# Identity products of TensorE in the first waits of six stages, and a tanh feed-forward stage that works on raw x with centred weights

## The chip, the cores and the metric

One core of a Trainium2 chip. A core has five engines that run their own instruction streams and meet through semaphores: TensorE (PE, matrix products; its weight loads are PEld in the profile), VectorE (DVE), ScalarE (ACT), GpSimd (POOL) and SyncE (SP, which only issues DMAs here). Operands lie in SBUF, products land in PSUM. The metric is the device time of one launch in microseconds; lower is better.

## The reference, cut to what matters

A residual stream `x` of 8 x 1024 tokens by 256 channels passes through eight sublayers, each fed with a layernorm of x without gain or offset. The change touches the arithmetic of the two tanh sublayers alone:

```python
def _layernorm(x, axis=-1, eps=1e-05):
    m = jnp.mean(x, axis=axis, keepdims=True)
    v = jnp.var(x, axis=axis, keepdims=True)
    return (x - m) / jnp.sqrt(v + eps)

def _L1_ffn_ref(x, weight, aux_weight1, aux_weight2, bias):
    h = jnp.einsum('btc,cd->btd', x, weight)
    h = jnp.einsum('btc,cd->btd', h, aux_weight1)
    h = jnp.einsum('btc,cd->btd', h, aux_weight2)
    return jnp.tanh(h + bias)

x = x + _L0_attn_a_ref(_layernorm(x), ...)   # local attention
x = x + _L0_ffn_ref(_layernorm(x), ...)      # top-k experts
x = x + _L0_attn_b_ref(_layernorm(x), ...)   # spectral attention
x = x + _L0_ffn_ref(_layernorm(x), ...)      # top-k experts again
x = x + _L1_attn_a_ref(_layernorm(x), ...)   # second-order attention
x = x + _L1_ffn_ref(_layernorm(x), ...)      # tanh stage, t6
x = x + _L1_attn_b_ref(_layernorm(x), ...)   # window attention
x = x + _L1_ffn_ref(_layernorm(x), ...)      # tanh stage, t8
```

Everything is float32.

## The kernel before, in words

x stays in SBUF as `R.X`, 64 tiles (NT) of 128 tokens by 256 channels. `hybrid_kernel` (L2627) calls one function for each sublayer, and a stage begins only when all engines have left the one before: each `nc.Block()` ends with all engines meeting. The statistics of each tile (`bn_stats` into `R.raw`) are taken by the stage that last writes it; the next stage turns them into `R.rstd` and `R.shift` in `layernorm_scales` (L73) on VectorE, with one square root on ScalarE (`std_of_var`, L91).

`tanh_ffn` (L149) runs twice, as `t6` and as `t8`, which also stores the output. Head of the stage: SyncE loads three 256x256 weights and the bias (L184, L185), all on one semaphore, `loaded`. TensorE waits for all four (L195), transposes the first weight into `psW` (L198), and multiplies twice (L209), so that `wc` holds the product of the three; ScalarE copies `psW` to SBUF between the steps (L236). Then come the 64 tiles. For each, VectorE normalizes the tile into `xn` (L259), TensorE transposes its two halves (L218) into one of two banks `psT`, ScalarE copies them to `xnT` (L242), TensorE multiplies them with `wc` (L226) into one of four banks `psY`, VectorE adds the bias (L266), ScalarE takes tanh (L248), GpSimd adds the result to x (L278), and in t6 VectorE takes the statistics (L270). `skewed` (L31) writes each engine's order: transposes of tile i, then products of tile i-2; on VectorE normalize i, bias i-3, stats i-7. The first and last tiles are written out, those between are a loop of four tiles with indices in registers. A float32 product of TensorE is two records in the trace, a transpose one.

The stages whose beginnings the change touches: the experts' second half (`top_k_experts`, L283; TensorE's order at L615), which waits for gathered rows (L581) and then multiplies (L596) for ScalarE's gelu (L644); `turned_copies` (L713), called only as `ww` for the weights of the window stage (transposes L739, copies L746); `spectral_attention` (L749), whose first products are L904 and which transposes its weights at L915; `second_order_attention` (L1463), which begins with a transpose (L1566) and products (L1573); `window_attention` (L1878), which begins with transposes of normalized tiles (L2017). In each of these TensorE's first instruction is a wait for a load or for a first tile.

## Time and profile before

| | us |
|---|---|
| median of 3 runs | 3975.1 (3974.56 to 3976.0) |
| the profiled execution | 3985.05 |
| span of its instructions | 3983.0 |
| PE busy in it | 3608.2 (91%) |
| DVE busy | 2388.3 (60%) |
| ACT busy | 2058.1 (52%) |
| POOL busy | 1351.3 (34%) |

Times in rows of the profile are microseconds from the start of the span; 2.05 us of the execution lie around the span. A row of the timeline gives the start, the duration, the engine, the line, the operation, what is written and what is read, how many were merged (x4), and in brackets how long the engine had stood idle and what ended that.
### The profile page before, as it was taken

Reading aid. Unit: us, or ns where it says so; the run is one execution under the profiler, and the core shown is the slowest. Engines: PE = TensorE matmul, PEld = TensorE weight load, DVE = VectorE, ACT = ScalarE, POOL = GpSimd, SP = SyncE. Lnnn points to the kernel's source line nnn. Section 1 sums busy time; section 2 is a strip of 40 time slices with the busy share of each in tenths; the row PEclk is TensorE's granted clock in tenths of the full one; section 3 lists DMA queues with packets and bytes.
Section 4 is the critical chain, followed back from the end, with each engine's and each line's share of the span. In section 5 each row is a group of like instructions: output and inputs, shape, how many; then the busy total and the mean of one; then the engine's idle time right before and its main releaser. Section 6 shows DMA issues by size and latency. Waiting matters only on the chain. (4 is left out here: it accounts for less than half of the span.)

```text
span 3983.0 us, 116418 instructions
## 1 busy us (share of the span) xinstructions
PE 3608.2 (91%) x44602; PEld 3108.5 (78%) x44602; DVE 2388.3 (60%) x6575; ACT 2058.1 (52%) x6294; POOL 1351.3 (34%) x1988
## 2 busy tenths in 40 slices
PE   8939999699739996999999999999987999999988
PEld 7829999577529996888888888888864777777766
DVE  6774554688665555344444444444446888888885
ACT  3335554455345552343434434444333788888884
POOL 3435565101036553333333333333324122222114
PEclk9969999899969998999999999999988999999998
DMA  3134444212144335000000000000000000000002
GB/s 116 44 132 99 90 95 95 86 48 61 49 151 92 90 78 135 2 3 3 3 3 3 3 3 3 3 3 2 3 11 15 2 2 2 2 2 2 2 2 94
DMA packets 137694, 162.36 MB, mean 41 GB/s; under 512 B 11329, under 2 KB 127969, under 8 KB 137185
## 3 DMA queue, kind: packets, MB, share of 16 engines
q1 hardware_dynamic: 112608, 121.71, 9.5%
q0 software_dynamic: 24576, 33.57, 4.9%
q8 instruction: 355, 5.82, 0.6%
q14 instruction: 155, 1.26, 0.1%
HBM read 96.39 MB, written 58.85 MB: 39 GB/s over the span
## 5 line engine op out<-in xcount | busy, mean ns | idle before, releaser
L2142 ACT ACTIVATE wa_S<-wa_S,wa_top 128x256 f32<-128x256 f32 x1024 | 511.6, 506 | 138.1 <-DVE wa_top L2206 137.2
L1801 DVE TENSOR_TENSOR so_AB<-so_rows,so_masks 128x1024 f32<-128x1024 f32 x256 | 313.6, 1225 | 246.4 <-PE so_rows L1545 227.4
L2206 DVE CUSTOM_DVE_ANT_0 wa_S<-wa_bank,wa_band 128x256 f32<-128x256 f32 x1024 | 366.9, 420 | 7.4 <-issue 7.3
L1860 POOL TENSOR_TENSOR so_state<-so_compact,so_head 128x384 f32<-128x384 f32 x224 | 185.1, 826 | 339.5 <-PE so_bankC L1612 248.3
L1790 DVE SCALAR_TENSOR_TENSOR so_compact<-so_compact,so_bankX 128x96 f32<-128x96 f32 x192 | 48.9, 255 | 414.2 <-PE so_bankX L1648 414.2
L2068 PE MATMUL wa_bank<-ident,wa_S 128*128 128x128 f32 x2048 | 275.1, 276 | 20.9 <-ACT wa_probT L2149 20.9
L2068 PEld LDWEIGHTS wa_bank<-ident,wa_S 128*128 128x128 f32 x2048 | 231.2, 141 | 66.0 <-ACT wa_S L2142 29.5
L1573 PE MATMUL so_bankJ<-so_xnT,so_w 128*128 128x128 f32 x2048 | 253.3, 278 | 1.2 <-ACT so_QT L1710 0.7
L1573 PEld LDWEIGHTS so_bankJ<-so_xnT,so_w 128*128 128x128 f32 x2048 | 242.1, 194 | 1.9 <-ACT so_QT L1710 1.0
L1736 ACT COPY so_OT<-so_bankC 128x128 f32<-128x128 f32 x256 | 68.1, 266 | 307.7 <-PE so_bankC L1612 307.7
L1855 POOL TENSOR_TENSOR so_Ug<-so_U,so_decay_t 128x128 f32<-128x128 f32 x224 | 102.1, 456 | 325.4 <-ACT so_U L1723 325.4
L644 ACT ACTIVATE m4e_hT<-m_bank,m4e_bias 128x256 fp32r<-128x256 f32 x256 | 127.4, 498 | 153.7 <-PE m_bank L596 147.9
L644 ACT ACTIVATE m2e_hT<-m_bank,m2e_bias 128x256 fp32r<-128x256 f32 x256 | 125.9, 492 | 149.5 <-PE m_bank L596 143.0
L2142 ACT ACTIVATION_READ_ACCUMULATOR wa_S<-wa_S,wa_top 128x1 f32 x1024 | 199.2, 195 | 0.0
L2214 DVE COPY wa_probT<-wa_bank 128x512 f32<-128x512 f32 x256 | 167.0, 687 | 48.0 <-PE wa_bank L2068 46.7
L596 PE MATMUL m_bank<-m2e_exT,m_w_parts 128*128 128x256 f32 x1536 | 190.7, 284 | 0.0
L596 PE MATMUL m_bank<-m4e_exT,m_w_parts 128*128 128x256 f32 x1536 | 190.1, 283 | 0.3 <-ACT m4e_h L644 0.3
L610 PE MATMUL m_bank<-m_w_parts,m4e_hT 128*128 128x256 f32 x1536 | 189.5, 282 | 0.6 <-DVE m4e_pre L691 0.6
L610 PE MATMUL m_bank<-m_w_parts,m2e_hT 128*128 128x256 f32 x1536 | 189.5, 282 | 0.6 <-DVE m2e_pre L691 0.6
L610 PEld LDWEIGHTS m_bank<-m_w_parts,m4e_hT 128*128 128x128 f32 x1536 | 186.3, 189 | 0.8 <-issue 0.8
L610 PEld LDWEIGHTS m_bank<-m_w_parts,m2e_hT 128*128 128x128 f32 x1536 | 186.3, 189 | 0.8 <-issue 0.8
L596 PEld LDWEIGHTS m_bank<-m2e_exT,m_w_parts 128*128 128x128 f32 x1536 | 185.1, 191 | 0.0
(427 smaller groups left out, 9889.4 us busy)
## 6 DMA issues: line engine op xcount, KB each, us to landing
m_w_raw<-in_L_ffn_W_dram SPq DMA_DIRECT2D x64, 512.0 KB, 3.7
sum_dram<-X SPq DMA_DIRECT2D x16, 1024.0 KB, 4.8
X<-sum_dram SPq DMA_DIRECT2D x16, 1024.0 KB, 7.3
X<-in_L_attn_a_x_dram SPq DMA_DIRECT2D x8, 1024.0 KB, 11.6
xn_dram<-m2r_xn SPq DMA_DIRECT2D x16, 512.0 KB, 3.1
sp_gx<-gate_dram SPq DMA_DIRECT2D x64, 128.0 KB, 2.9
xn_dram<-m4r_xn SPq DMA_DIRECT2D x16, 512.0 KB, 3.1
out_dram<-X SPq DMA_DIRECT2D x8, 1024.0 KB, 4.4
```

Source lines behind the costliest of these rows:

```text
L596: last = nc.tensor.matmul(bank[:, 0:2 * P], w_parts[:, par, a, c, f * P:(f + 1) * P], exT[:, s % 2, b, c], start=(n == 0), stop=(n == len( ...
L610: last = nc.tensor.matmul(by[u][:, 0:HID], hT[:, s % 2, a, f, u * P:(u + 1) * P], w_parts[:, par, b, 2 + f // QF, f % QF * HID:(f % QF + 1 ...
L644: last = nc.scalar.activation(to, bh[f % 4][:, 0:2 * P], ACT.Gelu_apprx_tanh, bias=bias[:, par, f:f + 1])
L1573: last = nc.tensor.matmul(bJ[:, k * P:(k + 1) * P], w[:, n, c, k * P:(k + 1) * P], xnT[:, c * P:(c + 1) * P], start=(c == 0), stop=(c == H ...
L1736: nc.scalar.copy(OT[:, t % (2 * UT)], bC[:, P:2 * P]).then_inc(s_["O_ready"], 1)
L1801: nc.vector.tensor_tensor(AB[:, t % 2].rearrange("p h m t -> p h (m t)"), rows4[:, :, 0:2 * P], masks[:].rearrange("p m t -> p (m t)")[:, ...
L1855: nc.gpsimd.tensor_tensor(Ug[:, t % 2], U[:, t % 2], decay_t[:], ALU.mult).then_inc(s_["Ug_ready"], 1)
L1860: nc.gpsimd.tensor_tensor(state[:, t % UT], compact[:, t % UT, :, None, :].broadcast_to([P, 3, HG, DK]), head[:, None, :, None].broadcast_ ...
L2068: last = nc.tensor.transpose(bT[q % 2][:, (2 * h + k) * P:(2 * h + k + 1) * P], S[:, n % 2, 2 * q + h, k * P:(k + 1) * P], R.ident[:])
L2142: nc.scalar.activation(S[:, n % 2, z], S[:, n % 2, z], ACT.Exp, bias=top[:, n % 2, z:z + 1], scale=-1.0, accum_out=sums[:, i % 2, SET * c ...
L2206: nc.vector.tensor_tensor_reduce(out=S[:, n % 2, z], in0=bS[g][:, eo * SPAN:(eo + 1) * SPAN], in1=band[:], scale=-(D ** -0.5), scalar=3e38 ...
L2214: nc.vector.tensor_copy(probT[:, n % 2, 2 * q:2 * q + 2].rearrange("p h k t -> p (h k t)"), bT[q % 2][:]).then_inc(s_["T_dve"], 1)
```

## The change

A helper, `keep_busy`, issues products of the 128x128 identity with itself into a bank that isn't in use yet. It is called as TensorE's first work in the experts' second half (30 products), in `turned_copies` (12), in the spectral (13), second-order (30) and window stage (30), and twice in the head of a tanh stage (6 and 4).

The tanh stage no longer normalizes x. The mean over its input channels is taken out of each column of the first weight (`off`, added while `psW` is copied to `wT`, now by VectorE), so that raw x times these weights equals centred x times the old ones; the division by the deviation is done behind the product, where VectorE multiplies by `R.rstd` and adds the bias in one operation. TensorE transposes tiles of `R.X` as they stand, from the block's beginning, in the order turn 0, fillers, weight transposes, turn 1, fillers, first weight product, turn 2, second, turn 3, then for each i products i and turn i+4. There are three banks for transposes and three for products (before two and four). Each weight has its own semaphore, and the bias is waited for by VectorE alone. All 64 tiles are written out, with no loop in registers.

```diff
@@ -93,6 +93,12 @@
     nc.scalar.activation(R.var[:], R.var[:], ACT.Sqrt).then_inc(std_ready, 1)
 
 
+def keep_busy(nc, R, bank, count):
+
+    for _ in range(count):
+        nc.tensor.matmul(bank[:, 0:P], R.ident[:], R.ident[:], start=True, stop=True)
+
+
...
 
 
@@ -151,6 +157,7 @@
     def sem(name):
         return sem_(f"{tag}_{name}")
 
+    RING, AHEAD = 4, 4
...
@@ -162,27 +169,29 @@
         wT = sb("wT", [P, HC, HID])
         w01T = sb("w01T", [P, HC, HID])
         wc = sb("wc", [P, HC, HID])
+        off = sb("off", [P, HC])
         bias_all = sb("bias_all", [P, HID])
-        xn = sb("xn", [P, 4, HID])
-        xnT = sb("xnT", [P, 4, HC, P])
+        xT = sb("xT", [P, RING, HC, P])
         pre = sb("pre", [P, 4, HID])
         th = sb("th", [P, 4, HID])
-        psT = [ps(f"psT{i}", [P, 512]) for i in range(2)]
-        psY = [ps(f"psY{i}", [P, 512]) for i in range(4)]
+        psT = [ps(f"psT{i}", [P, 512]) for i in range(3)]
+        psY = [ps(f"psY{i}", [P, 512]) for i in range(3)]
         psW = ps("psW", [P, HC, HID])
 
...
 
         with nc.Block() as block:
             @block.sync
             def _(sp):
                 for n, src in enumerate((weight, aux1, aux2)):
-                    sp.dma_start(w[:, n], src.rearrange("(c p) d -> p c d", p=P)).then_inc(loaded, 16)
-                sp.dma_start(bias_all[:], bias.rearrange("(a d) -> a d", a=1).broadcast_to([P, HID])).then_inc(loaded, 16)
+                    sp.dma_start(w[:, n], src.rearrange("(c p) d -> p c d", p=P)).then_inc(w_loaded[n], 16)
+                sp.dma_start(bias_all[:], bias.rearrange("(a d) -> a d", a=1).broadcast_to([P, HID])).then_inc(bias_loaded, 16)
...
@@ -191,93 +200,112 @@
 
             @block.tensor
             def _(pe):
-
-                pe.wait_ge(loaded, 64)
+                def turn(i):
+                    if i >= len(psT):
+                        pe.wait_ge(xT_ready, i - len(psT) + 1)
+                    for c in range(HC):
+                        last = nc.tensor.transpose(psT[i % len(psT)][:, c * P:(c + 1) * P], R.X[:, i, c * P:(c + 1) * P], R.ident[:])
+                    last.then_inc(psT_ready, 1)
+
+                def products(i):
+                    pe.wait_ge(xT_ready, i + 1)
+                    if i >= len(psY):
+                        pe.wait_ge(pre_ready, i - len(psY) + 1)
+                    for c in range(HC):
+                        last = nc.tensor.matmul(psY[i % len(psY)][:, 0:HID], xT[:, i % RING, c, :], wc[:, c, :], start=(c == 0), stop=(c == HC - 1))
+                    last.then_inc(psY_ready, 1)
+
+                turn(0)
+                keep_busy(nc, R, psY[0], 6)
+                pe.wait_ge(w_loaded[0], 16)
                 for c in range(HC):
                     for h in range(HC):
                         last = nc.tensor.transpose(psW[:, h, c * P:(c + 1) * P], w[:, 0, c, h * P:(h + 1) * P], R.ident[:])
                 last.then_inc(wstep, 1)
-                for m, (lhs, rhs) in enumerate(((1, wT), (2, w01T))):
-
-                    pe.wait_ge(wcopied, m + 1)
-                    for o in range(HC):
-                        for c in range(HC):
-                            if m == 0:
-                                a, b = w[:, 1, c, o * P:(o + 1) * P], wT[:, c, :]
-                            else:
-                                a, b = w01T[:, c, o * P:(o + 1) * P], w[:, 2, c, :]
-                            last = nc.tensor.matmul(psW[:, o, :], a, b, start=(c == 0), stop=(c == HC - 1))
-                    last.then_inc(wstep, 1)
-                pe.wait_ge(wcopied, 3)
-
-                def transposes(i, s):
-                    pe.wait_ge(xn_ready, i + 1)
-                    if past(i, 2):
-                        pe.wait_ge(xnT_ready, i - 1)
+                turn(1)
+                keep_busy(nc, R, psY[0], 4)
+                pe.wait_ge(w_loaded[1], 16)
+                pe.wait_ge(wT_ready, HC)
+                for o in range(HC):
                     for c in range(HC):
...
-                    last.then_inc(psT_ready, 1)
-
-                def products(i, s):
-                    pe.wait_ge(xnT_ready, i + 1)
-                    if past(i, 4):
-                        pe.wait_ge(pre_ready, i - 3)
+                        last = nc.tensor.matmul(psW[:, o, :], w[:, 1, c, o * P:(o + 1) * P], wT[:, c, :], start=(c == 0), stop=(c == HC - 1))
+                last.then_inc(wstep, 1)
+                turn(2)
+                pe.wait_ge(w_loaded[2], 16)
+                pe.wait_ge(wcopied, 1)
+                for o in range(HC):
                     for c in range(HC):
-                        last = nc.tensor.matmul(psY[s][:, 0:HID], xnT[:, s, c, :], wc[:, c, :], start=(c == 0), stop=(c == HC - 1))
-                    last.then_inc(psY_ready, 1)
-
-                skewed(pe, NT, [(0, transposes), (2, products)], unroll=4)
+                        last = nc.tensor.matmul(psW[:, o, :], w01T[:, c, o * P:(o + 1) * P], w[:, 2, c, :], start=(c == 0), stop=(c == HC - 1))
+                last.then_inc(wstep, 1)
+                turn(3)
+                pe.wait_ge(wcopied, 2)
+                for i in range(NT):
+                    products(i)
+                    if i + AHEAD < NT:
+                        turn(i + AHEAD)
 
             @block.scalar
             def _(act):
+                def copy_xT(i):
+                    act.wait_ge(psT_ready, i + 1)
+                    if i >= RING:
+                        act.wait_ge(psY_ready, i - RING + 1)
+                    nc.scalar.copy(xT[:, i % RING].rearrange("p c t -> p (c t)"), psT[i % len(psT)][:, 0:HID]).then_inc(xT_ready, 1)
+
+                def tanh(i):
+                    act.wait_ge(pre_ready, i + 1)
+                    if i >= 4:
+                        act.wait_ge(x_ready, i - 3)
+                    nc.scalar.activation(th[:, i % 4], pre[:, i % 4], ACT.Tanh).then_inc(th_ready, 1)
+
                 std_of_var(nc, act, R, var_ready, std_ready)
-                for m, dst in enumerate((wT, w01T, wc)):
-                    act.wait_ge(wstep, m + 1)
-                    nc.scalar.copy(dst[:], psW[:]).then_inc(wcopied, 1)
-
...
+                copy_xT(0)
+                copy_xT(1)
+                act.wait_ge(wstep, 2)
+                nc.scalar.copy(w01T[:], psW[:]).then_inc(wcopied, 1)
+                copy_xT(2)
+                act.wait_ge(wstep, 3)
+                nc.scalar.copy(wc[:], psW[:]).then_inc(wcopied, 1)
+                copy_xT(3)
+                for i in range(NT):
+                    if i + AHEAD < NT:
+                        copy_xT(i + AHEAD)
+                    tanh(i)
 
             @block.vector
             def _(dve):
                 layernorm_scales(nc, dve, None, R, step, var_ready, std_ready)
-
-                def normalize(i, s):
-                    if past(i, 4):
-                        dve.wait_ge(psT_ready, i - 3)
-                    nc.vector.tensor_scalar(xn[:, s], row_of(R.X, i), R.rstd[:, bass.ds(i, 1)], R.shift[:, bass.ds(i, 1)],
-                                            ALU.mult, ALU.add).then_inc(xn_ready, 1)
-
-                def add_bias(i, s):
+                dve.wait_ge(wstep, 1)
+                nc.vector.tensor_reduce(off[:], psW[:], AX_X, ALU.add).then_inc(centred, 1)
+                dve.wait_ge(centred, 1)
+                nc.vector.tensor_scalar(off[:], off[:], -1.0 / HID, None, ALU.mult).then_inc(centred, 1)
+                dve.wait_ge(centred, 2)
+                for h in range(HC):
+                    nc.vector.tensor_scalar(wT[:, h, :], psW[:, h, :], off[:, h:h + 1], None, ALU.add).then_inc(wT_ready, 1)
+                dve.wait_ge(bias_loaded, 16)
+
+                def add_bias(i):
                     dve.wait_ge(psY_ready, i + 1)
-                    if past(i, 4):
+                    if i >= 4:
                         dve.wait_ge(th_ready, i - 3)
-                    nc.vector.tensor_tensor(pre[:, s], psY[s][:, 0:HID], bias_all[:], ALU.add).then_inc(pre_ready, 1)
-
-                def stats(i, s):
+                    nc.vector.scalar_tensor_tensor(out=pre[:, i % 4], in0=psY[i % len(psY)][:, 0:HID], scalar=R.rstd[:, i:i + 1],
+                                                   in1=bias_all[:], op0=ALU.mult, op1=ALU.add).then_inc(pre_ready, 1)
+
+                def stats(i):
                     dve.wait_ge(x_ready, i + 1)
-                    nc.vector.bn_stats(row_of(R.raw, i), row_of(R.X, i))
-
-                skewed(dve, NT, [(0, normalize), (3, add_bias)] + ([(7, stats)] if out is None else []), unroll=4)
+                    nc.vector.bn_stats(R.raw[:, i, :], R.X[:, i, :])
+
+                for i in range(NT + 4):
+                    if i < NT:
+                        add_bias(i)
+                    if out is None and i >= 4:
+                        stats(i - 4)
 
             @block.gpsimd
             def _(pool):
-                def residual(i, s):
+                for i in range(NT):
                     pool.wait_ge(th_ready, i + 1)
-                    nc.gpsimd.tensor_tensor(row_of(R.X, i), row_of(R.X, i), th[:, s], ALU.add).then_inc(x_ready, 1)
-
-                skewed(pool, NT, [(0, residual)], unroll=4)
+                    nc.gpsimd.tensor_tensor(R.X[:, i, :], R.X[:, i, :], th[:, i % 4], ALU.add).then_inc(x_ready, 1)
 
 
 def top_k_experts(nc, R, tag, A, C, before):
@@ -612,6 +640,7 @@
                                                         start=(n == 0), stop=(n == len(steps) - 1))
                         last.then_inc(down_done, 1)
 
+                    keep_busy(nc, R, ban[5], 30)
                     skewed(pe, PAIRS, [(0, turn_x), (1, up), (2, down)], unroll=U)
 
                 @block.scalar
@@ -731,6 +760,7 @@
 
             @block.tensor
             def _(pe):
+                keep_busy(nc, R, banks[0], 12)
                 pe.wait_ge(loaded, 16 * len(jobs))
                 for n, (parts, _) in enumerate(blocks):
                     if n >= 2:
@@ -1058,6 +1088,7 @@
                     pe.wait_ge(L_copied, u + 1)
                     nc.tensor.transpose(yb[1][:, HID:HID + P], turned_L[:], R.ident[:]).then_inc(LT_done, 1)
 
+                keep_busy(nc, R, fb[0], 13)
                 pe.wait_ge(c_loaded, 48)
                 for b in range(2):
                     for n in range(TB // 2):
@@ -1649,6 +1680,7 @@
                                                 V[:, tile(t) % 2, t % UT, head_rows(h)], start=True, stop=True, tile_position=(0, h * DK))
                     last.then_inc(s_["S_done"], 1)
 
+                keep_busy(nc, R, bC, 30)
                 pe.wait_ge(s_["loaded"], 9 * 16)
                 turn_x(0)
                 project(0, 0)
@@ -1997,6 +2029,7 @@
 
             @block.tensor
             def _(pe):
+                keep_busy(nc, R, bO, 30)
                 pe.wait_ge(s_["loaded"], 5 * 16)
                 pe.wait_ge(s_["zeroed"], 5)
 
```

## Rows read from the trace of the kernel before

**Rows 1.** The page: TensorE's granted clock in 40 slices, tenths.

```profile
PEclk9969999899969998999999999999988999999998
```

**Rows 2.** Stretches of the tanh loops: length, busy PE, PEld, DVE, ACT, POOL, then PEclk, DMA.

```profile
2958.13:3038.43 80.30, 75.24 (x375) 54.82 (x375) 65.53 (x180) 43.69 (x125) 43.55 (x60) 0.99 0.00 0
3900.37:3975.35 74.98, 74.44 (x375) 55.52 (x375) 51.16 (x122) 43.70 (x125) 43.59 (x60) 0.99 0.29 98
```

**Rows 3.** Timeline: head of t6, and t8's first product.

```profile
2940.27 0.38 SPq L184 DMA_DIRECT2D t_w<-in_L_ffn_weight_dram  x1
...
2945.74 1.11 PE L198 MATMUL t_psW<-ident,t_w 128*128 128x128 f32 x4 [9.50 <-DMA t_bias_all<-in_L_ffn_bias_dram]
2946.89 0.58 ACT L236 COPY t_wT<-t_psW 128x512 f32<-128x512 f32 x1 [4.43 <-PE t_psW L198]
...
2947.53 3.78 PE L209 MATMUL t_psW<-t_wT,t_w 128*128 128x256 f32 x8 [0.67 <-ACT t_wT L236]
...
2958.13 1.91 PE L226 MATMUL t_psY<-t_wc,t_xnT 128*128 128x256 f32 x4
...
3900.37 1.92 PE L226 MATMUL t_psY<-t_wc,t_xnT 128*128 128x256 f32 x4
```

**Rows 4.** DMA issues in the head: size, median us to landing.

```profile
t_w<-in_L_ffn_weight_dram SPq DMA_DIRECT2D x1, 256.0 KB, 2.8
```

**Rows 5.** Timeline: products of neighbouring tiles, and of t6's last three.

```profile
2961.31 1.03 PE L226 MATMUL t_psY<-t_wc,t_xnT 128*128 128x256 f32 x4
...
2962.40 1.03 PE L226 MATMUL t_psY<-t_wc,t_xnT 128*128 128x256 f32 x4
...
3036.71 2.76 PE L226 MATMUL t_psY<-t_wc,t_xnT 128*128 128x256 f32 x12
```

**Rows 6.** Waits in t6's loop: total us, times, longest.

```profile
PEld t_psT L218 <- DVE t_xn L259: 12.2, 39, 0.6
```

**Rows 7.** Groups of instructions: count, busy us, mean ns, idle before.

```profile
L1372 DVE SCALAR_TENSOR_TENSOR sp_late<-sp_gx,sp_bank 128x256 f32<-128x256 f32 x64 | 25.8, 420 | 20.4 <-PE sp_bank L1023 19.5
...
L436 DVE TENSOR_REDUCE m2r_Lsum<-m2r_L 128x64 f32<-128x512 f32 x1 | 0.7, 686 | 0.0
```

**Rows 8.** Short stretches, columns as in the group of the tanh loops.

```profile
2960.00:2962.00 2.00, 2.00 (x13) 1.74 (x11) 1.45 (x4) 0.84 (x3) 0.00 (x0) 0.95 0.00 0
...
753.00:757.00 4.00, 0.19 (x2) 0.00 (x0) 0.61 (x2) 4.00 (x9) 0.00 (x0) 0.77 0.00 0
...
735.00:737.00 2.00, 2.00 (x20) 2.00 (x19) 1.83 (x4) 1.42 (x3) 2.00 (x17) 1.00 0.00 0
```

**Rows 9.** Timeline: beginnings of the other stages, first real work of each.

```profile
296.21 0.20 DVE L667 TENSOR_SCALAR m2e_bias<-m_b 128x8 f32<-128x8 f32 x1 [2.23 <-PEq L118]
...
306.12 1.12 PE L581 MATMUL m_bank<-ident,m2e_ex_in 128*128 128x128 f32 x4 [13.21 <-DMA m2e_ex_in<-xn_dram,m2e_rows]
...
716.72 0.27 DVE L77 TENSOR_TENSOR mean<-raw 128x64 f32<-128x64 f32 x1 [2.60 <-PEq L118]
...
722.44 6.39 PE L904 MATMUL sp_bank<-sp_dft,sp_xn 128*128 128x128 f32 x32 [30.54 <-ACT sp_xn L1130]
...
733.40 5.84 PE L915 MATMUL sp_bank<-ident,sp_late 128*128 128x128 f32 x52
...
1580.36 0.27 DVE L77 TENSOR_TENSOR mean<-raw 128x64 f32<-128x64 f32 x1 [2.60 <-PEq L118]
...
1590.88 0.66 PE L1566 MATMUL so_bankJ<-ident,so_xn 128*128 128x128 f32 x2 [35.34 <-POOL so_xn L1840]
...
1592.06 3.79 PE L1573 MATMUL so_bankJ<-so_xnT,so_w 128*128 128x128 f32 x16 [0.52 <-ACT so_xnT L1703]
...
3042.00 0.37 SPq L730 DMA_DIRECT2D ww_staged<-in_L_attn_b_Wqkv_dram  x1
...
3047.48 3.76 PE L739 MATMUL wa_bank<-ident,ww_staged 128*128 128x128 f32 x16 [8.01 <-DMA ww_staged<-in_L_attn_b_Wout_dram]
...
3063.69 2.20 PE L2017 MATMUL wa_bank<-ident,wa_xn 128*128 128x128 f32 x8 [12.45 <-POOL wa_xn L1961]
```

22 lines of the change are left out of this document (6 added, 16 removed).

## The prediction

> **What bounds the kernel now.** I read the page's clock line first [rows 1], and its busy shares, then the busy table of the two tanh stages [rows 2], then the beginning of the first of them instruction by instruction [rows 3, 4], then two neighbouring tiles and the last ones [rows 5], then the waits [rows 6]. TensorE carries the kernel: it is at full clock in most slices, and busy for 91% of the span, so time is won where TensorE waits, or where it works at 1.2 GHz instead of 2.4. The diff touches both.
>
> In a tanh stage the two windows of rows 2 run from the first product of tile 0 to the first product of tile 63. The end points are worked out from the timeline: 2958.13 and 3900.37 begin the first products [rows 3], and the last three tiles are one run of twelve records from 3036.71 [rows 5], of which the last tile has four, so tile 63 begins 8 x 0.215 = 1.72 us later, at 3038.43. (The second stage's 3975.35 is read in the same way.) So 63 tiles take 80.3 us in the first stage (1.27 us each) and 75.0 us in the second (1.19). VectorE is busy for 65.5 and 51.2 us of them, ScalarE for 43.7, GpSimd for 43.6 [rows 2]. VectorE has three operations per tile in the first stage (normalize, add bias, stats) and register work between them; TensorE's weight loads wait 12.2 us for the normalized tile there, the largest wait of TensorE in the loop [rows 6]. Where TensorE isn't held up, as in the tiles before the loop, a tile takes 1.085 us from products to products (2961.31 to 2962.40, and the pair before it alike) [rows 5]: 4 x 0.215 for the products, the rest for two transposes.
>
> The head of the stage is a chain: loads issued at 2940.27, TensorE's first work at 2945.74 (it waits for the bias, which it doesn't need), transposes, copy, 3.78 us of products, copy, 3.78 us, copy, the first transposes of x, the first product at 2958.13 [rows 3]. All of it runs at 1.2 GHz; the clock comes back at about 2960.1 (0.95 granted in 2960 to 2962) [rows 8].
>
> **The tanh stages, per tile.** *Normalize* leaves VectorE: 64 operations, and their register work and waits. The bias addition becomes one operation that multiplies by the reciprocal deviation and adds. No such instruction with this shape reads a product here; the nearest, a three-operand one of 128x256 with one operand in PSUM, takes 0.42 us [rows 7], what the addition takes now. I take 0.42; even at 0.5 VectorE would have 0.92 us per tile with the stats, under TensorE's 1.085. ScalarE keeps a copy and a tanh (43.7/63 = 0.69 us) and GpSimd its addition (43.6/60 = 0.73) [rows 2]. So the next bound is TensorE's own 1.085 us. The new order puts the transposes of tile i+4 behind the products of tile i, with four turned tiles kept; the copy that a product needs was then issued three tiles earlier, over 3 us, which covers copy plus tanh. The last four tiles have no transposes: 0.86 each. From product 0 to product 63: 60 x 1.085 + 3 x 0.86 = 67.7 us, against 80.3 and 75.0: 12.6 and 7.3 us less. The tail behind the last product (bias, tanh, addition, store or stats) stays.
>
> **The tanh stages, head.** The bias no longer gates. The first weights land 2.8 us after issue [rows 4], at 2943.1. Till then TensorE turns tile 0 (0.45) and runs 6 fillers. A filler is a 128-column product in two records; at 1.2 GHz sixteen such records take 3.79 us with their end [rows 9], so a filler is about 0.43 us, at 2.4 GHz 0.215. 2940.3 + 0.45 + 2.6 = 2943.3. The four transposes of the weights end at 2944.5. The copy is replaced on VectorE by a reduction of 512 values (0.69 [rows 7]), a scaling (0.2, as small operations of VectorE take, 0.20 and 0.27 in rows 9) and two shifts of 0.42, with hand-overs 1.9 us instead of 0.58; its scales are done before. TensorE fills this with tile 1 and 4 fillers (2.2 us): first weight product at 2946.5, 1.0 us earlier than now. By then TensorE has worked some 6 us almost unbroken. Now TensorE's bursts have pauses of 0.67 us between them, and the clock rises only behind three of them [rows 3, 8]; I expect it up by about 2947. Then both products of weights take 2.1 instead of 3.78, the copies 0.65 each: 2946.5 + 2 x (2.1 + 0.68) = 2952.1, and product 0 follows at once, since tiles 0 to 3 are turned in the gaps. That is 6.0 us before 2958.13. If the clock stays low it is 2946.5 + 2 x (3.78 + 0.68) = 2955.4, 2.7 us. I take 6.0 in both stages.
>
> Tanh stages together: 12.6 + 7.3 + 12.0 = **31.9 us**.
>
> **The fillers of the other stages.** They gain only if the clock is still up when real work comes, if that work is bound by TensorE, and if they end before it. What fillers leave behind counts: from 753.2 TensorE stands still, and in 753 to 757 the grant averages 0.77, so it fell at about 755.2, 2 us after the last product [rows 8].
> - *Experts* (30 fillers, twice): block from 296.2, data at 306.12 [rows 9]. At 1.2 GHz throughout the fillers take 12.9 us and end 3 us late; with the rise after some 5 us they end near 305.1, with a pause of 1 us, the transposes (1.12 us at low clock) and again 1.6 us of waiting for VectorE. The clock will probably drop again in there. Sure is half of the transposes, 0.6 us. Behind them ScalarE's gelu is late, not TensorE. 0.6 each, bounds -2.9 and +1.5.
> - *Spectral* (13 fillers): 716.7 + 5.6 = 722.3 before 722.44 [rows 9]. Here the filler joins the work with hardly a pause, which is the good case: 32 records take 6.39 us, and would take 3.2 at 2.4 GHz. ScalarE and VectorE, which supply and empty, would hold them up then, and the clock still needs its first microseconds. 1.5 us, bounds 0 and 2.5.
> - *Second-order* (30): block from 1580.36, tile ready at 1590.88. Ends near 1589, then a pause of up to 2 us and bursts with waits. If the clock held, the 3.79 us of products at 1592.06 would halve, their equal twins behind them too, and the first round of the stage's small products with them, 5.5 us together; if it falls, 0 to 0.9. 0.8, bounds -2.2 and 5.5.
> - *Window weights* (12): 3042.0 + 5.2 = 3047.2, data used at 3047.48: almost no pause. Sixteen records take 3.76 us; ScalarE's copies of 0.59 come next, so 0.7, bounds -0.5 and 1.
> - *Window* (30): the tile comes 12.45 us after TensorE's last work [rows 9], a change of blocks included; its transposes are paced by GpSimd. 0.2, bounds -2 and 2.2.
>
> These sum to 1.2 + 1.5 + 0.8 + 0.7 + 0.2 = **4.4 us**.
>
> The Trainium skill (TensorE: Matmul & The Clock Gate, "Why this matters for your kernels") asks only that there be no long idle gaps between bursts. By that the pauses of 1 to 2 us behind the fillers would cost nothing, and second-order and window stages would gain their upper bounds. The 2 us of rows 8 speak against it, so I give that a rival and not the sum. The same page ("PE-mode transpose") states that transposes don't count as activity; the transposes from 733.40 run at 1.00 in 735 to 737 [rows 8, 9], so the trace doesn't bear that out, at least for holding the clock.
>
> **Sum.** 31.9 + 4.4 = 36.3 us. The profiled execution took 3985.05 us: 3948.7 there. The median, 3975.1, is 0.25% below it, so 3975.1 - 36.3 = **3938.8 us**.
>
> **Rivals.**
> 1. *The fillers hold the clock up into the real work* in second-order and window stages: +4.7 and +2.0. 3932. For it: only pauses of 1 to 2 us. Against: 755.2. Chance 0.13.
> 2. *The tile period stays near 1.19.* If something other than normalize sets the second stage's pace (TensorE is busy there for 74.4 of 75.0 us [rows 2], so it may simply be slower in long runs), the loop gains 5.3 and 0 instead of 12.6 and 7.3: 14.6 less, 3953. Against: the undisturbed tiles at 1.085. 0.12.
> 3. *The change doesn't do what it says*: fillers don't lift the clock. Heads 2.7 each (6.6 less), the other gains gone (4.4), and the long fillers end late: 2 x 2.9 + 2.2 + 2 = 10.0. Gain 15.3: 3960. Against: matrix products raise it everywhere else. 0.04.
> 4. *Slower than before*: the in-order queues close into a ring. ScalarE's copy for tile i+4 stands ahead of tanh i, TensorE's turn waits for a copy, and if that slack of three tiles isn't there a tile costs products, bias, tanh and copy in series: 1.03 + 0.42 + 0.42 + 0.37 = 2.2 us. 126 tiles x (2.24 - 1.085) = 146 less 36: 4085. It decides from a period of 1.085 + 36.3/126 = 1.37 on. Against: each wait reaches back three or four tiles. 0.02.
>
> The forecast itself has 0.69. Its own spread: heads 2.7 to 6.5, period 1.07 to 1.11 (3 us), and the spectral stage, where the clock falls and returns on its own; moving the start can add or remove a few such falls at 1.7 us each, so +-4. That gives 3931 to 3947.
>
> **Numbers.** 3938.8, range 3929 to 3952: it takes in rival 1 and leaves out half of 2, and 3 and 4. A measurement of this kernel tells about 0.2%, 8 us, from no change. Faster by more: 0.96; within: 0.02; slower: 0.02.
>
> **What would show it.** Right: products of neighbouring tiles 1.08 to 1.09 us apart in both stages and TensorE's wait for x gone; product 0 about 12 us after the first load's issue, with a grant of 1.00 by then; no idle of TensorE between fillers and the weights' transposes. Fillers: grant 1.00 at the end of each run, and 0.50 again while the second-order stage's first products run; if 1.00 there, rival 1. A period of 1.19 makes rival 2. The prediction is wrong if a real first instruction stands behind a running filler, or if TensorE waits for ScalarE's copy in the tanh loop.

## The result, and the profile after

The changed kernel takes 3945.57 us (median of 4 runs, 3944.08 to 3946.38), the kernel before 3975.55 beside it: a ratio of 0.9924, with a 95% interval from 0.9907 to 0.9941. That is 30.0 us less. The forecast had 3938.8, in a range from 3929 to 3952, and 36.3 less. The profiled executions differ by more than the medians: 3985.05 us before and 3945.89 after, 39.2 less. Where these 9 us come from is half of what follows.

The page of the changed kernel, its shares of busy time and TensorE's granted clock by slice:

```profile
PE 3624.8 (92%) x44932; PEld 3148.0 (80%) x44932; DVE 2352.1 (60%) x6455; ACT 2063.0 (52%) x6292; POOL 1352.5 (34%) x1988
...
PEclk9969999899969998999999999999999999999999
```

Beside [rows 1], the two 8s at three quarters of the span and the one at the end have gone. A slice is 99.6 us there. The first (2888 to 2987 us) and the last (from 3883) hold the heads of the two tanh stages, the second (2987 to 3087) the beginning of the window stage.

The table of busy time by stretch (start and end, length, busy PE, PEld, DVE, ACT, POOL with counts, PEclk, DMA share, GB/s) for the two tanh loops, again from the first product of tile 0 to the first of tile 63:

```profile
2943.00:3010.73 67.73, 67.73 (x372) 58.34 (x373) 49.23 (x120) 44.96 (x124) 44.08 (x61) 1.00 0.00 1
3868.68:3936.41 67.73, 67.73 (x372) 58.33 (x373) 30.00 (x62) 44.89 (x124) 44.03 (x61) 1.00 0.33 109
```

Against [rows 2] the stretches shrank from 80.30 and 74.98 to 67.73 us each: 12.57 and 7.25 less. TensorE is busy in all of it. In the waits of the first stretch no wait of TensorE for x or for its copy is left; VectorE, ScalarE and GpSimd now wait for TensorE or for each other. The columns are engine and line, what it waited for, total us, times, longest:

```profile
POOL X L308 <- ACT t_th L259: 43.9, 58, 23.8
DVE t_pre L291 <- PE t_psY L215: 24.0, 61, 6.8
ACT t_xT L253 <- PE t_psT L207: 21.6, 57, 1.2
...
PE t_psY L215 <- ACT t_wc L268: 0.5, 1, 0.5
```

The timeline of the first tanh stage's head (start, length, engine, line, operation, and in brackets the idle time before it and what ended it), to be read beside [rows 3]:

```profile
2931.86 0.38 SPq L193 DMA_DIRECT2D t_w<-in_L_ffn_weight_dram  x1
...
2931.91 0.66 PE L207 MATMUL t_psT<-ident,X 128*128 128x128 f32 x2 [4.08 <-PEq L124]
...
2932.36 2.64 PE L99 MATMUL t_psY<-ident 128*128 128x128 f32 x12
...
2934.90 0.66 PE L223 MATMUL t_psW<-ident,t_w 128*128 128x128 f32 x4
...
2935.61 1.06 PE L99 MATMUL t_psY<-ident 128*128 128x128 f32 x8
...
2936.60 0.88 DVE L284 TENSOR_SCALAR t_wT<-t_psW,t_off 128x256 f32<-128x256 f32 x2
...
2937.62 1.96 PE L231 MATMUL t_psW<-t_wT,t_w 128*128 128x256 f32 x8 [0.95 <-DVE t_wT L284]
...
2940.36 1.97 PE L238 MATMUL t_psW<-t_w,t_w01T 128*128 128x256 f32 x8 [0.55 <-ACT t_w01T L265]
...
2943.00 1.13 PE L215 MATMUL t_psY<-t_wc,t_xT 128*128 128x256 f32 x4 [0.46 <-ACT t_wc L268]
```

The weights' transposes (L223) follow the fillers without idle time, both weight products take 1.96 us instead of 3.78, and the first product stands 11.1 us after the first load was issued; before it was 17.9. The second stage has the same picture with its first product at 3868.68.

### The profile page after: what moved, and what is told of

It reads as the page before. It is cut to its first block and busy times, and to the rows that moved or that the text cites. A ratio compares the mean times of both kernels' runs of the same rounds, so it can differ in the third digit from the quotient of the medians.

```text
span 3944.1 us, 115809 instructions
## 1 busy us (share of the span) xinstructions
PE 3624.8 (92%) x44932; PEld 3148.0 (80%) x44932; DVE 2352.1 (60%) x6455; ACT 2063.0 (52%) x6292; POOL 1352.5 (34%) x1988
## 5 line engine op out<-in xcount | busy, mean ns | idle before, releaser
L624 PEld LDWEIGHTS m_bank<-m4e_exT,m_w_parts 128*128 128x128 f32 x1536 | 184.8, 190 | 0.0
## 6 DMA issues: line engine op xcount, KB each, us to landing
X<-in_L_attn_a_x_dram SPq DMA_DIRECT2D x8, 1024.0 KB, 11.8
```

The costliest lines, as they stand in the source:

```text
L624: last = nc.tensor.matmul(bank[:, 0:2 * P], w_parts[:, par, a, c, f * P:(f + 1) * P], exT[:, s % 2, b, c], start=(n == 0), stop=(n == len( ...
```

## Stages of the traces, side by side

Below, each trace is cut at landmarks of TensorE (the first operation of a stage, the last of its last tile), and the table gives the length of each piece in us. It is worked out from the timelines, so it is no row of the profile. The tanh pieces are head (up to the first product) and loop (from there to the issue of the next stage's load, or to the end). Two short pieces without much in them are left out (35 us ahead of the second-order stage, 21 ahead of the window stage). Landmarks are rounded to 0.1 us. The traces: A before, B before again, C before with the five stage fillers only, D tanh rewrite without fillers, E tanh rewrite with its head fillers, F after, G and H after a second and third time, I after with 36 fillers in the second-order stage, J the same and 48 in the window stage, K after without the expert fillers. The traces of experiments 6 to 8 aren't in the table; where they bear on a place, the text has their numbers.

```
trace                 A      B      C      D      E      F      G      H      I      J      K
local and route   306.1  306.1  304.1  303.9  302.9  303.2  306.0  303.7  304.0  304.9  303.7
experts 1         385.5  385.3  388.4  385.0  385.5  387.5  388.0  390.2  388.3  387.6  385.0
spectral, route   474.5  475.0  472.9  474.5  471.4  475.6  473.2  473.4  470.0  472.7  470.0
experts 2         389.2  389.0  385.2  388.5  388.2  386.5  385.1  386.2  385.2  386.3  387.5
second-order     1345.0 1344.9 1341.1 1341.1 1343.2 1339.5 1344.8 1339.4 1339.4 1339.5 1339.4
tanh 1, head       22.2   22.0   19.8   17.8   15.7   15.5   15.9   16.8   15.9   15.9   15.7
tanh 1, loop       83.9   83.9   82.8   71.2   71.2   71.3   71.3   71.3   71.3   71.3   71.3
window            814.7  819.1  816.1  816.4  817.7  817.1  817.8  818.9  816.9  813.0  814.7
tanh 2, head       22.0   20.1   20.0   18.1   16.1   15.9   16.2   16.1   16.0   15.8   15.9
tanh 2, loop       82.6   81.8   81.7   75.4   75.4   75.4   75.4   75.4   75.4   75.4   75.4
span             3983.0 3984.6 3970.2 3950.4 3944.7 3944.1 3951.4 3948.4 3939.2 3938.6 3935.5
```

The loops of the new tanh stages agree to 0.1 us in all traces. Other pieces of one and the same kernel differ by some us from trace to trace (F, G and H: second-order 1339.4 to 1344.8, local and route 303.2 to 306.0). Anything of that size is read below from the place where it arises, not from the span.

## The experiments

Each quotation stands as it was written before its run.

**1. The kernel before, once more.** No edit.

> The kernel before, unchanged, profiled once more. The two traces in hand differ by 38.9 us of span, the medians only by 30.0, because the profiled execution of before took 3985.05 us against a median of 3975.5. Theory A (that one execution was slow where TensorE's clock fell and rose at other moments, and in the waits on transfers): the new span is 3972 to 3976 us, and the 9 us are missing from the stages between the first experts and the window stage, not from the tanh loops, which again take 80.3 and 75.0 us from product 0 to product 63. Rival B (profiling itself costs this kernel 9 us, because of its loops in registers): the span is again 3981 to 3985 and the tanh loops are what the medians don't have.

Measured: 3977.38 us (11 runs, 3971.67 to 3986.56), ratio to the other runs of the same kernel 1.0002 (0.9992 to 1.0011); the profiled execution has a span of 3984.6 us. So the first profile was no single accident: both stand at the upper end, and the span of 3972 to 3976 that Theory A expected didn't come. Rival B, that being recorded costs this kernel 9 us because of its register loops, isn't borne out either: the kernel of experiment 4 has the same loops, and its recorded execution took 3972.04 us against a median of 3973.36. Of all 62 executions of the kernel before that were timed for these experiments, on several chips, 31 lie below 3975 us and 14 above 3979; the mean is 3975.8. In this trace the second head was shorter than in the first. Its second product of weights runs at 2.4 GHz:

```profile
3894.47 3.78 PE L209 MATMUL t_psW<-t_wT,t_w 128*128 128x256 f32 x8 [0.68 <-ACT t_wT L236]
3898.93 1.99 PE L209 MATMUL t_psW<-t_w,t_w01T 128*128 128x256 f32 x8 [0.68 <-ACT t_w01T L236]
```

It took 3.78 us in both heads of the first profile. The head is 20.1 us instead of 22.0. The saving that I read off a head of 22.2 is therefore 2 us smaller where the clock comes back one product earlier.

**2. The tanh rewrite without any filler.** All seven calls of the filler are left out:

```diff
-                keep_busy(nc, R, psY[0], 6)
...
-                keep_busy(nc, R, psY[0], 4)
...
-                keep_busy(nc, R, bC, 30)
```

> The new tanh stages with all calls of the filler helper left out, in the other stages and in the heads. Theory A (the arithmetic, not the fillers, carries the result): loops 12.6 and 7.3 us shorter, heads 2.7 each: 25 us faster than before, about 3950. Rival B (the fillers carry a third or more): only the loops' 20 us, 3956 or more, and the clock comes back 14 us after the stage's begin as in before.

Measured: 3952.22 us (5 runs), ratio 0.9936 (0.9922 to 0.9949). In the trace the loops have their full gain (71.2 and 75.4), and the heads are 17.8 and 18.1 us. The first product of weights is still slow, the second isn't:

```profile
2940.30 3.75 PE L229 MATMUL t_psW<-t_wT,t_w 128*128 128x256 f32 x8 [1.64 <-DVE t_wT L282]
...
2944.82 1.97 PE L236 MATMUL t_psW<-t_w,t_w01T 128*128 128x256 f32 x8 [0.34 <-ACT t_w01T L263]
```

So a head gains some 4 us on those of the first profile without any filler, where Theory A had 2.7 with the clock low throughout. By means, this kernel is 23.7 us below before (3952.1 against 3975.8, +-1.5 at two standard errors; all such figures below are at two standard errors). Four fifths of the whole gain need no filler.

**3. The tanh rewrite with its head fillers, the other five groups left out.**

> The new tanh stages with their head fillers (6 and 4), no filler in the other five places. Theory A: each head is 3.3 to 4 us shorter than without fillers, so 7 to 8 us faster than tanh_no_fillers, about 3943: as fast as the whole change or faster, the other five fillers being worth nothing in sum. Rival B (the second-order filler's 5.6 us seen in the trace are real and lasting): 5 us slower than the whole change, about 3950.

Measured: 3950.16 us (5 runs), ratio 0.9935 (0.9922 to 0.9949). The heads are 15.7 and 16.1 us, 2.1 and 2.0 shorter than without the fillers, which is the one product that now runs in 1.97 instead of 3.75 us. By the medians 2.1 us, by the means 1.2 +-3.1: the traces show these 4 us and the medians can't. Theory A had 3.3 to 4 us a head and about 3943 us in all; both were too much.

**4. The other five groups of fillers alone**, in the kernel before, its tanh stages untouched.

> The kernel before with the five filler calls outside the tanh stages and nothing else. Theory A (gains and losses of the five cancel): within 2 us of before, 3973 to 3978. Rival B (they bring what the two traces show, +5.6 in the second-order stage, -2.4 in the window stage, about +2 in the spectral head, nothing in the experts): 4 to 6 us faster, about 3970.

Measured: 3973.36 us (11 runs), ratio 0.9995 (0.9986 to 1.0004). The means give 2.5 us +-1.6 against all 62 executions of before. In the second-order stage the clock rose during the fillers, fell again at 1587.30 inside the first projection and rose at 1590.7; one projection takes 3.68 us and the other 2.05.

**5. The changed kernel once more.** No edit.

> The changed kernel once more, beside the same executions of before as the next three. Theory A (its time moves from execution to execution by where TensorE's clock falls and rises, as that of before does, from 3971 to 3987 us in the runs so far): 3943 to 3950, tanh loops of 63 tiles again 67.8 us in both stages, while the stages that the change doesn't rewrite move by 1 to 4 us each in either direction. Rival B (it is steady): within 1 us of 3945.6 and every stage within 1 us of the first trace.

Measured: 3948.02 us (5 runs, 3941.44 to 3953.24), ratio 0.9929 (0.9916 to 0.9942). The second-order stage takes 1344.8 us here and took 1339.5 in the first trace of the same kernel. Both timelines from the fillers on, first the first trace, where the clock held:

```profile
1577.88 9.40 PE L99 MATMUL so_bankC<-ident 128*128 128x128 f32 x60 [24.82 <-PEq L124]
1588.04 0.41 PE L1597 MATMUL so_bankJ<-ident,so_xn 128*128 128x128 f32 x2 [0.77 <-POOL so_xn L1872]
1588.97 2.05 PE L1604 MATMUL so_bankJ<-so_xnT,so_w 128*128 128x128 f32 x16 [0.52 <-ACT so_xnT L1735]
1591.70 2.05 PE L1604 MATMUL so_bankJ<-so_xnT,so_w 128*128 128x128 f32 x16 [0.68 <-ACT so_QT L1742]
```

Then this one, where it didn't:

```profile
1577.42 9.13 PE L99 MATMUL so_bankC<-ident 128*128 128x128 f32 x60 [24.83 <-PEq L124]
1588.70 0.54 PE L1597 MATMUL so_bankJ<-ident,so_xn 128*128 128x128 f32 x2 [2.15 <-POOL so_xn L1872]
1589.76 3.79 PE L1604 MATMUL so_bankJ<-so_xnT,so_w 128*128 128x128 f32 x16 [0.52 <-ACT so_xnT L1735]
1594.22 3.79 PE L1604 MATMUL so_bankJ<-so_xnT,so_w 128*128 128x128 f32 x16 [0.67 <-ACT so_QT L1742]
```

The clock rises earlier in the second (1582.0 against 1583.1), so the same 60 records end earlier (1586.55), and the x tile comes later: a pause of 2.15 us instead of 0.77. The table of stretches shows the fall, in 1588 to 1590:

```profile
1586.00:1588.00 2.00, 0.55 (x5) 0.36 (x4) 0.00 (x0) 0.00 (x0) 0.01 (x1) 1.00 0.07 19
1588.00:1590.00 2.00, 0.78 (x3) 0.44 (x4) 0.00 (x0) 0.37 (x1) 1.11 (x2) 0.71 0.00 0
1590.00:1592.00 2.00, 2.00 (x10) 2.00 (x11) 0.00 (x0) 0.00 (x0) 0.00 (x0) 0.50 0.04 8
```

From the first transpose to the stage's first small product it is 6.48 us in the one and 10.07 in the other, and the stage as a whole differs by 5.3. This is rival 1 of the prediction, with its size, in some executions and not in others. The same stretch takes 10.19 us in four of the six traces without fillers there, and 8.15 and 8.46 in the other two (D and experiment 8), where the clock came back by itself before the second projection.

**6 and 7. The changed kernel without the second-order fillers, and without the window stage's.** One line left out in each.

> The changed kernel without the 30 fillers of the second-order stage. Theory A (they hold the clock up into the first products, worth 5.6 us in the trace of after against that of before): the clock is low again when the first products come, the stage's beginning is 4 to 6 us longer, and the median rises by 3 to 5 us. Rival B (tanh_no_fillers, where the clock came back at 1592.8 without any filler, shows it to be chance): median within 1.5 us of after_again.

Measured: 3951.06 us (5 runs), ratio 0.9944 (0.9931 to 0.9957). Against the 14 executions of the changed kernel (mean 3946.6) its mean is 5.2 us higher, +-3.7; against the 5 of experiment 5, on the same chip, 4.3 +-5.0. In the trace the projections take 3.79 us each and the stretch above 10.19 us.

> The changed kernel without the 30 fillers of the window stage. Theory A (they are useless: they end 4 us before the first normalized tile, the clock falls in between, 3033.7, and is low for the first 8 us of real work): same as after_again within 1.5 us, and the clock comes back 4 to 9 us after the first real work. Rival B (by raising and dropping the clock they make it come back later, 8.2 us after the first work against 5.7 before): 1.5 to 2.5 us faster than after_again.

Measured: 3951.30 us (5 runs), ratio 0.9938 (0.9925 to 0.9951); mean 4.0 us higher, +-3.7. The place itself doesn't bear that out. From the first transposes of the window stage to the next ones it is 11.30 us here (3044.42 to 3055.72), and 12.49, 12.24 and 12.65 in the three traces of the changed kernel. But without these fillers it also differs from trace to trace: 11.24, 12.92, 11.60, 12.24 and 12.77 us in A, B, D, E and the trace of experiment 8. The sixteen products between them take 8.53 us in A and 10.19 in B, where the clock rose 3.4 us later after the stage's first transposes:

```profile
3066.47 10.19 PE L2023 MATMUL wa_bank<-wa_xnT,wa_wT 128*128 128x512 f32 x16 [0.68 <-ACT wa_xnT L2134]
```

Over all traces it is 11.2 to 12.9 us without the fillers (mean 12.0, six traces) and 11.2 to 12.7 with 30 of them (mean 12.1, seven traces). They bring nothing here, and cost nothing.

The trace also has its first second-order projection at 3.79 us (the pause was 2.59 us), and a second tanh head of 18.2 us (17.6 in the trace without second-order fillers): there the weights landed 1.2 and 1.0 us after the fillers' end, and part of the first product of weights ran at 1.2 GHz (it took 2.80 us here). So the 4 us can't be put down to the window stage's fillers.

**8. The kernel before with its tanh loops written out.** Normalize stays; only the loop over a register goes, for all engines of the tanh stages:

```diff
-    if blocks < 2:
+    if flat or blocks < 2:
...
-                skewed(pe, NT, [(0, transposes), (2, products)], unroll=4)
+                skewed(pe, NT, [(0, transposes), (2, products)], unroll=4, flat=True)
```

> The kernel before with the tanh stages' loops written out for all 64 tiles on every engine, x still normalized by VectorE, no filler, nothing else changed. It parts two things that the change does at once. Theory A (my prediction's step: normalize on VectorE is what made a tile 1.27 and 1.19 us): the loops stay near 80 and 75 us from product 0 to product 63, at most 2 us less each. Rival B (the register work and the loop's waits made it so, not the operation; VectorE starts an operation every 0.36 us, three of them are 1.08): 67.7 to 70 us in both, so 16 to 19 us faster than before, nearly all that the rewritten loops gave.

Measured: 3973.32 us (12 runs, 3962.06 to 3979.93), ratio 0.9994 (0.9984 to 1.0004). The first loop is 80.1 us (83.9 before, 71.3 after), the second 76.1 (82.6 and 75.4). So the two loops lost their time to different things. In the first, VectorE's three operations still set the pace; tiles come at turns of 1.09 and 1.38 us, and TensorE waits for the normalized tile:

```profile
ACT t_xnT L242 <- PE t_psT L218: 27.5, 51, 0.7
...
PEld t_psT L218 <- DVE t_xn L259: 16.6, 50, 0.5
```

In the second, with two operations on VectorE, tiles follow at 1.09 us, a few at 1.17, once the register loop is gone, with normalize in place. Of the 7.2 us there some 6 belong to the way the loop was written, and of the 12.6 in the first some 4.

**9 to 12. Four kernels on one chip: the changed kernel, longer fillers, no expert fillers.**

> The changed kernel once more, beside the three kernels below on the same chip. Theory M (the two tanh stages carry the change, and whether the second-order stage begins at 2.4 GHz differs from execution to execution): about 3946 to 3949 us, ratio to the kernel before 0.9925 to 0.9935; the first two 16-record projections of the second-order stage last either 2.05 or 3.79 us each, and the stage takes about 1340 us in the one case and 1345 in the other. Theory N (a fixed gain, and the differences between the traces so far have to do with something else): the same stage length as in the two traces of the changed kernel only by chance.

Measured: 3946.05 us (5 runs), ratio 0.9925 (0.9911 to 0.9939). The second-order stage begins fast (2.05 us twice, stage 1339.4), with a pause of 1.70 us behind the fillers.

```diff
-                keep_busy(nc, R, bC, 30)
+                keep_busy(nc, R, bC, 36)
```

> The changed kernel with 36 instead of 30 fillers ahead of the second-order stage, so that they end some 1.3 us later, right at its first real work. Theory M (the clock is lost in the pause between the fillers' end and the first transposes, 0.77 us in one trace of the changed kernel where it held and 2.15 us in the other where it fell): the pause goes to under 1 us, the clock holds through the first transposes and both projections last 2.05 us; the stage takes 1339 to 1341 us in the trace. Where the executions of the changed kernel hold it about half the time, the median falls by 0 to 5 us, most likely 2 to 3. Theory N (the pause doesn't matter): the clock falls as in the second trace of the changed kernel, both projections last 3.79 us, and the six further fillers cost up to 1 us.

Measured: 3945.51 us (5 runs), ratio 0.9925 (0.9911 to 0.9939). The 72 records end 0.54 us before the x tile is there, and the clock holds:

```profile
1572.63 10.89 PE L99 MATMUL so_bankC<-ident 128*128 128x128 f32 x72 [24.83 <-PEq L124]
1584.07 0.41 PE L1597 MATMUL so_bankJ<-ident,so_xn 128*128 128x128 f32 x2 [0.54 <-POOL so_xn L1872]
1585.00 2.05 PE L1604 MATMUL so_bankJ<-so_xnT,so_w 128*128 128x128 f32 x16 [0.52 <-ACT so_xnT L1735]
```

It held in the next kernel too (pause 0.17 us). But with 30 fillers it held after pauses of 0.77, 1.70 and 2.41 us and fell in or after pauses of 1.42, 2.15 and 2.59. The length of the pause alone doesn't decide it, and two traces with 36 that held could be luck. The means differ by 1.8 us +-3.6: not settled.

In the fourth kernel the 30 fillers of the window stage (bank bO) become 48 as well.

> As the kernel with 36 fillers in the second-order stage, and with 48 instead of 30 ahead of the window stage, where the 30 end 4.15 us before the first transposes and the clock falls between. Theory M: the 48 end at the first transposes, the clock is at 2.4 GHz there and holds; the stage's product that took 9.77 us in the trace of the changed kernel takes some 5 to 6 us, and the window stage's beginning gets 2 to 5 us shorter, if GpSimd and VectorE, which prepare its operands, let it; against the kernel with 36 alone -1 to -4 us. Theory N (the beginning of the window stage is bound by the engines that prepare its operands): the clock is up but the stage's length is within 1 us of the other traces (815 to 818).

Measured: 3943.49 us (5 runs, 3939.05 to 3948.56), ratio 0.9920 (0.9906 to 0.9934). First the changed kernel at this place, then the one with 48:

```profile
3024.65 6.94 PE L99 MATMUL wa_bank<-ident 128*128 128x128 f32 x60 [1.36 <-PEq L124]
3035.74 2.21 PE L2050 MATMUL wa_bank<-ident,wa_xn 128*128 128x128 f32 x8 [4.15 <-POOL wa_xn L1993]
3038.62 9.77 PE L2056 MATMUL wa_bank<-wa_xnT,wa_wT 128*128 128x512 f32 x16 [0.68 <-ACT wa_xnT L2167]
3048.23 1.04 PE L2050 MATMUL wa_bank<-ident,wa_xn 128*128 128x128 f32 x8
```

```profile
3023.35 10.96 PE L99 MATMUL wa_bank<-ident 128*128 128x128 f32 x96 [1.36 <-PEq L124]
3034.43 1.95 PE L2050 MATMUL wa_bank<-ident,wa_xn 128*128 128x128 f32 x8
3037.06 7.13 PE L2056 MATMUL wa_bank<-wa_xnT,wa_wT 128*128 128x512 f32 x16 [0.68 <-ACT wa_xnT L2167]
```

With 30 there are 4.15 us of idle time, the clock falls at 3033.7 and the sixteen products take 9.77 us (8.53 and 10.19 in the two traces of before). With 48 the gap is closed and they take 7.13, the full-speed value of the next tile. From transposes to transposes it is 9.60 us against 12.49, 2.9 less, and the stage takes 813.0 us against 817.1 to 818.9. Against the six traces without fillers (11.2 to 12.9 us) it is 1.6 to 3.3 less, in this one trace. The median is the lowest of the study; by means it is 3.5 us below the changed kernel, +-3.7, so a gain over it isn't proven.

The fifth kernel leaves out the fillers ahead of both expert stages.

> The changed kernel without the 30 fillers ahead of each of the two expert stages. The forecast had 0.6 us of gain for each, so 1.2 us more here. Theory M (ScalarE's gelu, not TensorE, is late behind the first transposes): the stages from their first transposes to their last turned hidden tile keep their length within the scatter of the traces (385 to 390 us each), and the median is within 1.5 us of the changed kernel's. Rival: the fillers take power or clock from the stage behind them, and without them the first expert stage is 2 to 3 us shorter (385 to 386 instead of 387.5 to 390.4 as in the traces with fillers); then this kernel is 1 to 2 us faster.

Measured: 3945.23 us (5 runs), ratio 0.9927 (0.9913 to 0.9940); mean 2.0 us below the changed kernel, +-4.2. The first expert stage takes 385.0 us, as in all traces without these fillers (385.0 to 385.5), against 387.5 to 390.4 in those with them. The second goes the other way, 387.5 to 389.2 without them and 385.1 to 386.5 with (trace by trace, those of experiments 6 to 8 included). The rival of that expectation has the right number for the first stage and the wrong one for the second. Together they come to about nothing.

The fillers do bring something at the first stage's beginning: from its first transposes to the first product that reads a turned hidden tile it is 17.61 us before and 15.62 after. That lead is lost far behind, 274 us into the stage. First the trace of after there, then that of before at the same tile:

```profile
577.15 0.63 PE L609 MATMUL m_bank<-ident,m2e_ex_in 128*128 128x128 f32 x4 [2.03 <-issue]
```

```profile
578.83 0.60 PE L581 MATMUL m_bank<-ident,m2e_ex_in 128*128 128x128 f32 x4
```

TensorE stands still for 1.6 to 2.1 us at this tile in all eight traces with the fillers and in none of the six without; the gathered rows had landed at 574.75, 2.4 us before. The second stage has the same stop of 1.4 to 2.0 us, 272 to 276 us in, in all fourteen traces. In the first stage TensorE also waits, in sum, 0.8 to 2.5 us for gathered rows in those eight traces, against 0 to 0.6 in the others. What stops it at that tile the trace doesn't show ("issue"), and why the fillers bring it on stays open. The clock isn't the reason: in the trace of after the grant is 1.00 from 299.64 to 695.59.

## Why the prediction was right, and where its sum was not

**The loops: right to the tenth.** 67.7 us from product 0 to product 63 was forecast, 67.73 was measured in both stages, with neighbouring products 1.085 us apart (2944.18, 2945.27, 2946.35). Rival 2 is out. VectorE's new operation takes 0.48 us, not 0.42, which is hidden as the prediction said it would be up to 0.5. The prediction was mistaken that no such instruction reads a product in the kernel before; local attention has one of the same form, with a factor for each partition, and its 476 ns are near (behind the first bar stand busy us and mean ns):

```profile
L2552 DVE SCALAR_TENSOR_TENSOR X<-la_ps_o,la_share,X 128x256 f32<-128x256 f32 x64 | 30.4, 476 | 0.2 <-issue 0.2
```

The reason given for the second stage was wrong: the prediction let normalize carry both. Experiment 8 shows that the register loop carried 6 of the 7.2 us there. The change removes both, so the term came out right for half a reason.

**The heads: the mechanism right, the base mis-sized.** 6.0 us each was forecast; between the two profiles it is 6.7 and 6.1. The clock was up at 2934.7, earlier than the 2947 of the forecast (2.9 us after the load's issue, not 6.7), and the product stood 11.1 us after the issue instead of 11.8. But the head of before that I priced is its long form. With the same code it was 20.1 in the second trace of before and 19.8 and 20.0 in trace C; over all traces with that code it ranges from 19.8 to 22.4. Measured against the short ones, the gain is 4 us a head. Without fillers the heads are 17.8 and 18.1 us, so against the heads of the first profile some 4 of the 6 us came from the new order and some 2 from the fillers, where the prediction had 2.7 and 3.3. I took the one profiled execution for the typical one. Its loops and heads together are 210.7 us; in trace B 207.8, in trace C 204.3.

**The fillers.** 4.4 us was forecast, and the means of experiment 3 and of the changed kernel differ by 4.3 +-3.3 (experiment 4 has 2.5 +-1.6 for the same five groups). Place by place, in the trace of after: spectral 2.0 (the stretch from its first product to its transposes shrank from 10.96 to 8.98 us; forecast 1.5; it is 8.98 to 9.20 in all nine traces with these fillers and 10.23 to 11.26 in the five without), window weights 0.2 (0.7), the beginnings of the experts up to their first products 0.9 and 0.2 (0.6 each, and lost again in the first stage), window about 0 by all traces (0.2), second-order 5.5 or about 0 (0.8). The window weights' fillers met a clock that hadn't fallen yet: the twelve took 2.92 us instead of 5.2 and ended 2.54 us before the data, where the forecast had almost no pause. In traces I and J the pause was 0.71 and 1.23 us, and the sixteen transposes took 2.48 us instead of 3.53.

The second-order stage is the term that I weighed wrongly. I let one fall, 2 us after TensorE stood still [rows 8], decide against a hold over pauses of that length, and gave rival 1 a chance of 0.13. In the six traces with 30 fillers there, the clock held in three and fell in three, by the start of the first projection. The stage takes 1341.2 us on average in these six and 1343.4 in the six without fillers, so the term was worth some 2 us on average. The Trainium skill (TensorE: Matmul & The Clock Gate, "Why this matters for your kernels") asks for no long idle gap between bursts of products. By it all six would have held. The window stage agrees with it where the 4.15 us gap lost the clock and closing it kept it; but in traces C, H and K the pause ahead of that stage's transposes was only 2.50, 2.81 and 2.58 us, and the clock fell all the same as these ended, at 3055.03, 3039.98 and 3031.97.

**The rest of the gap, 36.3 against 30.0.** The sum was made against an execution of 3985.05 us and then moved to a median 0.25% lower, as if both kernels' medians stood equally far below their traces. For the kernel before they do (mean of 62 executions 3975.8, profiles 3985.05 and 3986.56); for the changed one the profile of 3945.89 stands among its 14 executions (mean 3946.6). So 36.3 should have been checked against a typical execution, not an unlucky one. Two places of it are seen in the traces: the heads, 2 to 4 us too long, and the second-order stage, 1345.0 us in both traces of before, where the kernels without fillers there range from 1341.1 to 1345.0. That is up to 8 of the 9 to 10 us by which the traces' gain exceeds the means' 29.2 (+-1.9). It is worked out, not shown: no execution of before near 3972 us was profiled, and the rest stays open.

**The other rivals.** Rival 3 (fillers don't lift the clock) is out: in the trace of after the grant is 1.00 at the end of each group but the second tanh stage's, where it rises at 3863.16, just ahead of the first product of weights (3863.30). Rival 4 (a ring of queues) is out: TensorE waits for ScalarE's copy nowhere in the loop. The other sign of being wrong, a real instruction behind a running filler, came up in small size: in the trace of after the weights' transposes begin 0.04 us after the landing, but in the first tanh head of traces G, I and J 0.34 to 0.39 us after it.

## What to carry to other kernels

Take the pace of an undisturbed pair of iterations as the forecast for a loop whose bottleneck is removed; it was good to 0.1 us in 68. Do not price a start-up, nor judge a filler there, from one trace: look at the same place in several executions, with and without, for the clock comes back a product earlier or later, and each such step is 1.8 us here. A filler has to reach up to the real work: where it ended 4.15 us early it brought nothing, where it ended at the work it gained, and where the pause was 1 to 2.5 us it was a draw from execution to execution. Before pricing a new instruction, look for one of its exact form in the trace.

## What was not expected of the hardware

The clock's rise isn't tied to the number of fillers. It came 5.2, 4.6 and 3.9 us after the first of the second-order fillers in the three traces of the changed kernel, so the same 60 records took 9.40, 9.13 and 8.78 us and ended at different distances from the work. A group of fillers sized by time at 1.2 GHz thus ends early by a different amount each time. And the same program has executions from 3971.2 to 3986.6 us (before) and 3941.4 to 3953.2 us (after), a spread of 0.3 to 0.4%. Part of it is where the clock falls and rises at the stage changes, as in the second-order stage (1339.4 to 1344.8 us with one kernel); the rest wasn't traced.
